# Dividing the attention output by its denominators: from transposed tiles to compacted ones with spread reciprocals

## The chip, the core and the metric

The kernel runs on one core of a Trainium2 chip. Its engines run side by side, each in the order of its own instructions: TensorE (PE) multiplies matrices and writes PSUM; VectorE (DVE) and ScalarE (ACT) read PSUM and work elementwise; GpSimd (POOL) works on SBUF; SyncE (SP) issues the DMA transfers, in order. They meet at semaphores. The metric is the device time of one execution in microseconds (us), the median of several runs.

## What is computed

One layer for 16 batches of 256 tokens with 512 features: cross attention with 32 heads of 16 features over 256 context tokens, then a feed-forward part. Cut to what matters here:

```
q = rope(layernorm(x) @ Wq);  k = rope(ctx @ Wk);  v = ctx @ Wv
w = softmax(q k^T / 4)                        # per head, 32 heads
attn = w @ v                                  # 16 x 256 x 512
x = x + tanh(g_x) * (attn @ Wout + bout)
h = square(relu(layernorm(x) @ up))
y = h @ down + (x_n @ expert) * (sum of the two largest of x_n @ gate)
out = x + tanh(g_f) * (layernorm(y) * gamma + beta)
```

All products keep about float32 accuracy: each operand is split into a rounded part (hi) and the rest (lo), and three products hi*hi, lo*hi, hi*lo are summed (`PASSES`).

## The kernel before

There are two stages: attention, batch by batch, and the feed-forward part in blocks of 512 tokens. The attention stage is a software pipeline: iteration i (from -1 to 15) has 16 steps, and in each step TensorE computes logits twice for a pair of heads: `logits_a` for batch i+1 (into pA, for the maxima, which VectorE takes and which the next step's `logits_a` waits for) and `logits_b` for batch i (into pB, transposed and with the maxima subtracted inside the product; ScalarE's Exp follows). Every second step `times_v` multiplies the exponentials of four heads by the values and a column of ones: pO then holds, for head j of the group, 16 rows of numerators at partition 32j and the denominator in row 32j+16. ScalarE copies it to `av_s` [128, 8 groups, 256] (`take_av`).

The rest of a step's work is jobs by name, from the table `SCHEDULE`; `LAG` says which batch a job works on (i+2, i+1, i or i-1) and `BANK` which of three PSUM banks (P, M, T) it uses. A bank is used by its jobs in turn: a job waits until the last one there was taken. X0 and X1 turn normalised x on TensorE, K, Q, V are projections, kT and qT turn the rotated keys and queries, m0 and m1 the maxima; O0 and O1 are the output products of the two halves of the tokens. A name with "<" is the first half of a product that is cut in two. VectorE and ScalarE empty a job's bank one step after it was computed. After K and Q, VectorE does two products with the rope tables and GpSimd adds them (`rope_sum`), before kT or qT can turn the sum. In the opening batches 0 and 1 are prepared (`OPENING`); iterations 14 and 15 have no jobs for batch i+2 left, and in iteration 15 the first tiles of the feed-forward stage are normalised and turned.

Around the change: per batch, four jobs a00, a10, a01, a11 turn `av_s` (four transposes of 128x128 each) so that tokens lie on partitions; VectorE takes the reciprocals of 16 denominators per token and multiplies them in, giving `attn`. Jobs aT0 and aT1 turn `attn` back (four transposes each), ScalarE rounds and VectorE subtracts, giving `aT` for O0 and O1. a00 stands in step 15 of its own iteration, the others in the next one.

SyncE issues per iteration: the stacks `stk` and `stq` (keys and queries laid out for the logits, four groups of six transfers), the maxima (two groups of four), x, context, the residual `xres`, and the store of x1, in the order written in `iteration` of the SyncE part. `first_loads` brings the first tiles and weights of the feed-forward stage in iteration 15.

## Time and profile before

| | |
|---|---|
| median of 3 runs | 1601.75 us (1600.06 to 1601.91) |
| the profiled execution | 1600.03 us, span 1598.2 us |
| TensorE busy | 1542.5 us (97%) |
| VectorE, ScalarE, GpSimd busy | 976.6 (61%), 638.5 (40%), 295.7 us (19%) |
| opening and iteration 0 | to 105 us |
| iterations 1 to 13 | 105 to 688 us, 44.88 us each |
| iterations 14 and 15 | 36.9 and 35.9 us |
| feed-forward stage | from 761 us |

Shares are averages over stages with different limits; a change in the attention stage is read from that stage's own rows. A timeline row has its start, its length, the instruction with what it writes and reads, the number of merged instructions, and in brackets the idle time before it with what ended it. Lengths of neighbouring TensorE rows overlap, since products are pipelined; what a job displaces is the distance between starts.

### The profile page before, as it was taken

To read this page: it belongs to the slowest core of one execution; us is meant where nothing else is said; L and a number is where in the kernel's file an instruction comes from. 1 tells how busy PE (TensorE), PEld (TensorE's weight loads), DVE (VectorE), ACT (ScalarE), POOL (GpSimd) and SP (SyncE) were. 2 spreads that over 40 slices of the span, in tenths; PEclk is the share of its full clock that TensorE was granted. 3 is DMA by queue.
4 is the path that set the end of the run, shared out by engine and by line. 5 is a ranking of instruction groups with operands and counts; after the bars stand their busy time and mean duration, and the time that the engine had idled before them with its cause. 6 is when DMAs were issued, how large, how long until landed. Compare 5 with 4: busy or idle time off the path is not lost.

```text
span 1598.2 us, 26049 instructions
## 1 busy us (share of the span) xinstructions
PE 1542.5 (97%) x9818; PEld 1157.1 (72%) x9818; DVE 976.6 (61%) x1448; ACT 638.5 (40%) x962; POOL 295.7 (19%) x370
## 2 busy tenths in 40 slices
PE   8799999999999999988999999999999999999997
PEld 6466666666666666655787887888878878788886
DVE  7887777878877777865662535436444354353524
ACT  3365555555655555566442222222222222222221
POOL 5212222222221222201010201002011020010202
PEclk9799999999999999999999999999999999999999
DMA  6644444445544334433530101101001011010101
GB/s 173 142 114 103 106 102 114 116 113 128 128 114 109 103 100 112 99 97 98 166 114 1 54 27 33 38 11 53 27 27 33 21 48 33 12 48 21 50 4 40
DMA packets 67192, 121.24 MB, mean 76 GB/s; under 512 B 12280, under 2 KB 25720, under 8 KB 67064
## 3 DMA queue, kind: packets, MB, share of 16 engines
q1 hardware_dynamic: 67064, 119.50, 27.9%
q8 instruction: 84, 1.38, 0.4%
q14 instruction: 44, 0.36, 0.1%
HBM read 51.17 MB, written 16.78 MB: 43 GB/s over the span
## 4 chain that ended last, share of the span: by engine, by line
PE 84%; DVE 11%; issue 2%; ACT 1%; POOL 1%; DMA 0%; POOLq 0%; DVEq 0%; ACTq 0%; SPq 0%
PE pP L986 16%; PE pA L1183 11%; PE pO L986 11%; PE pB L1183 11%; PE pT L986 9%; PE pO L1108 6%; PE pA L1080 6%; DVE mneg L1402 5%; PE pM L986 4%; PE pB L1096 2%; PE pT L993 2%; PE pP L993 2%; PE pM L993 2%; PE pM L1150 1%; DVE xn L1291 1%
## 5 line engine op out<-in xcount | busy, mean ns | idle before, releaser
L1402 DVE TENSOR_REDUCE mneg<-pA 128x4 f32<-128x1024 f32 x250 | 305.6, 1222 | 136.4 <-PE pA L1080 134.6
L887 ACT ACTIVATE probs<-pB 128x1024 f32<-128x1024 f32 x249 | 255.2, 1025 | 257.8 <-PE pB L1096 247.6
L1505 DVE TENSOR_TENSOR relu<-relu 128x512 f32<-128x512 f32 x128 | 88.4, 691 | 250.2 <-ACT hid L939 250.1
L704 POOL TENSOR_SCALAR var_eps<-meanvar 128x1 f32<-128x1 f32 x96 | 34.5, 360 | 1039.3 <-DVE meanvar L1287 1039.1
L1183 PE MATMUL pA<-dn,hid 128*128 128x512 f32 x768 | 196.9, 392 | 1.2 <-DVE hid L1507 1.0
L1183 PE MATMUL pB<-dn,hid 128*128 128x512 f32 x768 | 195.0, 389 | 0.0
L986 PE MATMUL pP<-fT,up 128*128 128x512 f32 x768 | 188.5, 394 | 0.0
L986 PE MATMUL pO<-fT,up 128*128 128x512 f32 x768 | 185.0, 390 | 0.0
L1183 PEld LDWEIGHTS pA<-dn,hid 128*128 128x128 f32 x768 | 143.0, 188 | 33.8 <-DVE hid L1507 4.5
L986 PEld LDWEIGHTS pO<-fT,up 128*128 128x128 f32 x768 | 143.9, 188 | 30.5 <-issue 0.5
L1183 PEld LDWEIGHTS pB<-dn,hid 128*128 128x128 f32 x768 | 144.2, 188 | 30.0
L986 PEld LDWEIGHTS pP<-fT,up 128*128 128x128 f32 x768 | 142.0, 188 | 29.8
L1080 PE MATMUL pA<-stk,stq 48*128 48x256 f32 x1000 | 127.9, 334 | 22.3 <-DVE mneg L1402 19.8
L1080 PEld LDWEIGHTS pA<-stk,stq 48*128 48x128 f32 x1000 | 76.0, 188 | 90.8 <-issue 57.8
L1108 PE MATMUL pO<-probs,v 128*17 128x256 f32 x2048 | 135.4, 382 | 2.1 <-ACT probs L887 2.1
L932 ACT ACTIVATE relu<-pO 128x512 f32<-128x512 f32 x64 | 38.3, 598 | 239.7 <-PE pO L986 239.7
L932 ACT ACTIVATE relu<-pP 128x512 f32<-128x512 f32 x64 | 38.3, 598 | 192.1 <-PE pP L986 192.1
L1096 PE MATMUL pB<-stq,stk 50*128 50x256 f32 x996 | 100.7, 280 | 0.0
L986 PE MATMUL pT<-wo,aT 128*128 128x512 f32 x384 | 99.1, 400 | 0.1
L986 PE MATMUL pT<-ex,fT 128*128 128x512 f32 x384 | 92.3, 389 | 0.0
L1507 DVE TENSOR_TENSOR hid<-relu,hid 128x512 fp32r<-128x512 f32 x128 | 88.6, 692 | 4.4
L986 PE MATMUL pP<-wq,xnT 128*128 128x512 f32 x336 | 90.6, 405 | 0.0
(199 smaller groups left out, 1972.8 us busy)
## 6 DMA issues: line engine op xcount, KB each, us to landing
stk<-kT SPq DMA_DIRECT2D x180, 128.0 KB, 2.9
stq<-qT SPq DMA_DIRECT2D x180, 128.0 KB, 3.0
fres<-x_scratch SPq DMA_DIRECT2D x34, 256.0 KB, 2.8
xin<-x SPq DMA_DIRECT2D x32, 256.0 KB, 3.0
xres<-x SPq DMA_DIRECT2D x32, 256.0 KB, 3.2
x_scratch<-xres SPq DMA_DIRECT2D x32, 256.0 KB, 2.3
out<-y_s SPq DMA_DIRECT2D x32, 256.0 KB, 2.0
fx<-x_scratch SPq DMA_DIRECT2D x29, 256.0 KB, 2.7
```

The source lines that it names most:

```text
L704: nc.gpsimd.tensor_scalar_add(var_eps[:], meanvar[:, 1:2], EPS).then_inc(ve_made, 1)
L887: nc.scalar.activation(probs[:, s % 4, :, :, :].rearrange("p a b s -> p a (b s)"), psum[:, :, :], ACT.Exp).then_inc(exp_done, 1)
L932: nc.scalar.activation(relu[m % 2][:], pU[m % 2], ACT.Relu).then_inc(relu_made, 1)
L986: last = nc.tensor.matmul(dst, lhs(a, c), rhs(w, c), start=(c == 0 and (a, w) == PASSES[0]), stop=(c == chunks_ - 1 and (a, w) == PASSES[-1]))
L993: last = nc.tensor.transpose(dst[:, c * P:(c + 1) * P], src(c), ident[:])
L1080: last = nc.tensor.matmul(psum[:, q, t * S:(t + 1) * S], st_q[par][rows, s, t * P:(t + 1) * P], st_k[par][rows, s, :], start=True, stop=True)
L1096: last = nc.tensor.matmul(psum[:, q, t * S:(t + 1) * S], st_k[par][rows, s, t * P:(t + 1) * P], st_q[par][rows, s, :], start=True, stop=True)
L1108: last = nc.tensor.matmul(pO[32 * j:32 * j + HD + 1, 0:S], v_s[par][:, t, 4 * g + j, :], probs[:, (2 * g + j // 2) % 4, j % 2, t, :], star ...
L1183: last = nc.tensor.matmul(acc[u], hid[m % 2][x_][:, u * P:(u + 1) * P], dn_s[w][:, m, :], start=(m == 0 and k == 0), stop=(m == MC - 1 and ...
L1402: nc.vector.tensor_reduce(mneg[par][:, :, 2 * u:2 * u + 2].rearrange("p t q -> p q t"), psum[:, :, :].rearrange("p q (t k) -> p q t k", t= ...
L1505: nc.vector.tensor_tensor(r[:], r[:], r[:], ALU.mult).then_inc(sq_made, 1)
L1507: nc.vector.tensor_tensor(hid[m % 2][1][:], r[:], hid[m % 2][0][:].bitcast(F32), ALU.subtract).then_inc(hid_lo, 1)
```

## The change

The division no longer goes through transposed tiles. For each batch and each half h of its groups (four groups, 16 heads):

- `gather_den`: one transfer collects the 16 heads' denominators from four partitions of `av_s` into `den` [64, 64].
- `reciprocals`: VectorE takes the reciprocal, rounds it and subtracts (den_hi, den_lo), at step 14 for the first half and step 3 of the next iteration for the second.
- `scatter_recips`: two transfers lay both parts out as 32 rows of 256 (`recips`).
- Job b0 or b1: two TensorE products of `spread`, a 0/1 tile made once on GpSimd in the opening (`make_spread`), with `recips`, which puts each head's reciprocal on the 16 partitions of its features.
- `move_av`: four transfers compact the numerators of `av_s` into `numer` (128 partitions, no gaps).
- VectorE multiplies b's bank into `numer`, ScalarE rounds (`round_av`, steps 4 and 8) and GpSimd subtracts (`rest_av`), giving `aT_hi` and `aT_lo`, which O0 and O1 use. The rows of Wout are permuted on the host to match.

The jobs a00, a10, a01, a11, aT0 and aT1 are gone. V1 moves from step 11 to step 4 and to bank T; O0 from steps 8 and 9 to 9 and 11, O1 from 13 to 13 and 15. GpSimd's order gets `rest_av` ahead of Q0's and of Q1's sum, the residual between. SyncE's order changes: `first_loads` stands before the second half's gather, the second part of stq after the residual, the store of the second x1 tile in the next iteration. In the first feed-forward block b0 stands at m = 0, b1 at m = 2, O0 and O1 at m = 3 and 4.

```diff
 SCHEDULE = {
-    0: ("X0", "a10"),
+    0: ("X0",),
-    2: ("Q0<", "a01"),
+    2: ("Q0<", "b0"),
...
+RECIPROCALS = {14: 0, 3: 1}
+ROUNDED = {4: 0, 8: 1}
...
+R_AT = HALF_ROWS
+R_ROWS = 2 * NH // 2
+MOVES = 4
...
-        attn = [sb1(f"attn{t}", [P, D]) for t in range(TT)]
-        aT = [sb1(f"aT{i}", [P, KC, P], F32R) for i in range(2)]
+        numer = under("numer", [P, KC, S])
+        aT_lo = sb1("aT_lo", [P, KC, S], F32R)
+        aT_hi = sb1("aT_hi", [P, KC, S], F32R)
...
-        rden = [sb1(f"rden{i}", [P, NH // 2]) for i in range(2)]
+        den = under("den", [HALF_ROWS, S // 4])
+        den_lo = sb1("den_lo", [HALF_ROWS, S // 4], F32R)
+        den_hi = sb1("den_hi", [HALF_ROWS, S // 4], F32R)
...
+        recips = low[0][R_AT:R_AT + R_ROWS, :]
+        spread = low[1][R_AT:R_AT + R_ROWS, :].rearrange("r (c p) -> r c p", c=2)
...
+            def gather_den(b, h):
+                sp.wait_ge(av_taken, GROUPS * b + GROUPS // 2 * (h + 1))
+                if some(2 * b + h):
+                    sp.wait_ge(rc_in, 2 * INC * (2 * b + h))
+                sp.dma_start(den[:, :], av_s[HD:P:32, GROUPS // 2 * h:GROUPS // 2 * (h + 1), :]
+                             .rearrange("j g (r s) -> j (g r) s", r=4)).then_inc(den_in, INC)
+            def scatter_recips(b, h):
+                sp.wait_ge(rc_made, 3 * (n + 1))
+                if some(n):
+                    freed, of = ("b0", b) if h else ("b1", b - 1)
+                    sp.wait_ge(done[BANK[freed]], number(freed, of))
+                for k, part in enumerate((den_hi, den_lo)):
+                    sp.dma_start(recips[NH // 2 * k:NH // 2 * (k + 1), :].bitcast(F32), part[:, :].bitcast(F32)).then_inc(rc_in, INC)
+            def move_av(b, h):
+                sp.wait_ge(av_taken, GROUPS * b + GROUPS // 2 * (h + 1))
+                if some(b):
+                    sp.wait_ge(done[BANK["O1"]], number("O1", b - 1))
+                for j in range(MOVES):
+                    sp.dma_start(numer[j:P:4, 2 * h:2 * h + 2, :].rearrange("p c s -> p (c s)"),
+                                 av_s[32 * j:32 * j + HD, GROUPS // 2 * h:GROUPS // 2 * (h + 1), :]
+                                 .rearrange("d g s -> d (g s)")).then_inc(moved[h], INC)
...
+                if within(bt):
+                    move_av(bt, 0)
+                if ending:
+                    first_loads()
                 if within(b1) and not opened("kT1", b1):
                     load_stack(b1, (par + 1) % 2, 1, "k")
+                if within(bt):
+                    gather_den(bt, 1)
+                if within(bt - 1):
+                    store_x1(bt - 1, 1)
+                if within(bt):
+                    move_av(bt, 1)
+                    scatter_recips(bt, 1)
+                if within(i):
+                    load_max(i, par % 2, 1)
+                if within(bt):
+                    load_residual(bt)
...
+                gather_den(i, 0)
...
+                scatter_recips(i, 0)
...
+            def rest_av(b, h):
+                pool.wait_ge(at_hi, 2 * b + h + 1)
+                nc.gpsimd.tensor_tensor(aT_lo[:, cut, :], numer[:, cut, :], aT_hi[:, cut, :].bitcast(F32),
+                                        ALU.subtract).then_inc(at_lo, 1)
...
+            def round_av(b, h):
+                act.wait_ge(taken[BANK[f"b{h}"]], number(f"b{h}", b))
+                nc.scalar.copy(aT_hi[:, cut, :], numer[:, cut, :]).then_inc(at_hi, 1)
...
-                    u = int(name[1])
-                    pe.wait_ge(av_taken, GROUPS * b + GROUPS // 2 * (t + 1))
-                    last = turn(psum, lambda c: av_s[:, GROUPS // 2 * t + c, u * P:(u + 1) * P])
+                    pe.wait_ge(rc_in, 2 * INC * (2 * b + t + 1))
+                    for c in range(2):
+                        last = nc.tensor.matmul(psum[:, c * S:(c + 1) * S], spread[:, c, :], recips,
+                                                start=True, stop=True)
...
-                    nc.vector.reciprocal(r[:], heads[:, :, HD]).then_inc(rd_made, 1)
...
+                    dve.wait_ge(moved[t], MOVES * INC * (b + 1))
+                    nc.vector.tensor_tensor(numer[:, cut, :], psum.rearrange("p (c s) -> p c s", c=2), numer[:, cut, :],
+                                            ALU.mult).then_inc(freed, 1)
+            def reciprocals(b, h):
+                n = 2 * b + h
+                dve.wait_ge(den_in, INC * (n + 1))
+                nc.vector.reciprocal(d, d).then_inc(rc_made, 1)
+                nc.vector.tensor_copy(den_hi[:, :], d).then_inc(rc_made, 1)
+                nc.vector.tensor_tensor(den_lo[:, :], d, den_hi[:, :].bitcast(F32), ALU.subtract).then_inc(rc_made, 1)
...
+                    if s in RECIPROCALS and within(i - RECIPROCALS[s]):
+                        reciprocals(i - RECIPROCALS[s], RECIPROCALS[s])
```

Three places in the new order. SyncE at the boundary between two full iterations (stk, stq: stacks; mT, low: maxima; xres: residual; x_scratch: stored x1). Before, from the maxima of m0 on, over the boundary:

```order
L526 DMA stq<-mT 1x8x256 x4
L517 DMA stq<-qT 16x2x1024 x6
L542 DMA x_scratch<-xres 128x512
L517 DMA stk<-kT 16x2x1024 x6
L517 DMA stq<-qT 16x2x1024 x6
L498 DMA xin<-x 128x512
L537 DMA xres<-x 128x512 x2
L526 DMA stq<-mT 1x8x256 x4
L498 DMA xin<-x 128x512
```

And after, from the same place:

```order
L577 DMA stq<-low 1x8x256 x4
L540 DMA stq<-qT 16x2x1024 x6
L560 DMA low<-den_hi 16x4x64
L560 DMA low<-den_lo 16x4x64
L568 DMA numer<-av_s 32x1x512 x4
L540 DMA stk<-kT 16x2x1024 x6
L549 DMA den<-av_s 64x1x64
L593 DMA x_scratch<-xres 128x512
L568 DMA numer<-av_s 32x1x512 x4
L560 DMA low<-den_hi 16x4x64
L560 DMA low<-den_lo 16x4x64
L577 DMA stq<-low 1x8x256 x4
```

Two scatters and four moves now stand ahead of the next iteration's stk, and the gather of the second half's denominators behind it.

VectorE from the statistics in step 2 to Q0's rotation in step 4 (mneg: maxima, L1402 before and L1516 after). Before:

```order
L1282 BN_STATS stats<-xin 128x6
L1287 BN_AGGR meanvar<-stats 128x2
L1402 TENSOR_REDUCE mneg<-pA 128x2x2
L1347 RECIPROCAL rden<-pT 128x16
L1349 TENSOR_TENSOR attn<-pT,rden 128x256
L1291 TENSOR_SCALAR xn<-xin,meanvar,rstd 128x512
L1402 TENSOR_REDUCE mneg<-pA 128x2x2
L1333 TENSOR_TENSOR mT<-pM,mT 16x256
L1327 TENSOR_TENSOR rot_q<-pP,cos_t 128x512
L1330 TENSOR_TENSOR rot<-pP,sin_t 128x512
```

After:

```order
L1393 BN_STATS stats<-xin 128x6
L1398 BN_AGGR meanvar<-stats 128x2
L1516 TENSOR_REDUCE mneg<-pA 128x2x2
L1454 TENSOR_TENSOR numer<-pT,numer 128x512
L1402 TENSOR_SCALAR xn<-xin,meanvar,rstd 128x512
L1462 RECIPROCAL den<-den 64x64
L1464 CAST den_hi<-den 64x64
L1466 TENSOR_TENSOR den_lo<-den,den_hi 64x64
L1516 TENSOR_REDUCE mneg<-pA 128x2x2
L1444 TENSOR_TENSOR low<-pM,low 16x256
L1438 TENSOR_TENSOR rot_q<-pP,cos_t 128x512
L1441 TENSOR_TENSOR rot<-pP,sin_t 128x512
```

The product into numer takes the place of a reciprocal and a product; the three denominator operations stand between the normalisation and the maxima of step 4.

SyncE in iteration 15, around the first loads of the feed-forward stage. Before:

```order
L542 DMA x_scratch<-xres 128x512
L537 DMA xres<-x 128x512 x2
L595 DMA g_gamma<-gamma 128x512
L596 DMA g_beta<-beta 128x512
L597 DMA gt_raw<-gate 128x4x8
L599 DMA fx<-x_scratch 128x512
L599 DMA fres<-x_scratch 128x512 x2
L599 DMA relu<-x_scratch 128x512
L582 DMA y_s<-up 128x4x128 x4
```

After:

```order
L560 DMA low<-den_lo 16x4x64
L568 DMA numer<-av_s 32x1x512 x4
L661 DMA g_gamma<-gamma 128x512
L662 DMA g_beta<-beta 128x512
L663 DMA gt_raw<-gate 128x4x8
L665 DMA fx<-x_scratch 128x512
L665 DMA fres<-x_scratch 128x512 x2
L665 DMA relu<-x_scratch 128x512
L648 DMA y_s<-up 128x4x128 x4
L549 DMA den<-av_s 64x1x64
L593 DMA x_scratch<-xres 128x512
L568 DMA numer<-av_s 32x1x512 x4
```

The residual has gone behind, four moves stand ahead, and the gather, the scatter and the maxima of m1 follow the loads.

## Rows read from the trace of the kernel before

**Rows 1.** Windows; columns as named: stretch, engines' busy us, granted clock, DMA share.

```profile
core 0: us, PE busy (x) PEld busy (x) DVE busy (x) ACT busy (x) POOL busy (x), PEclk, DMA share, GB/s
40.00:80.00 40.00, 28.73 (x185) 19.13 (x183) 32.31 (x37) 12.55 (x20) 12.05 (x13) 0.74 0.68 142
...
419.12:464.00 44.88, 43.88 (x382) 29.69 (x382) 35.63 (x51) 25.36 (x36) 11.20 (x12) 1.00 0.45 114
688.41:725.32 36.91, 32.27 (x320) 20.56 (x321) 24.98 (x30) 22.04 (x30) 2.52 (x2) 1.00 0.35 95
725.32:761.26 35.94, 29.64 (x291) 17.71 (x291) 20.24 (x38) 24.37 (x37) 5.70 (x10) 1.00 0.36 106
```

**Rows 2.** Timeline of TensorE in iteration 7 and 8: start, length in us, instructions.

```profile
405.99 0.66 PE L993 MATMUL pT<-ident,attn 128*128 128x128 f32 x4
406.40 1.64 PE L986 MATMUL pM<-wv,ctx 128*128 128x512 f32 x6
407.97 0.50 PE L1080 MATMUL pA<-stk,stq 48*128 48x256 f32 x4
...
409.63 0.39 PE L1058 MATMUL pM<-ident,mneg 128*16 128x128 f32 x2
409.85 0.60 PE L993 MATMUL pP<-ident,rot_q 128*128 128x128 f32 x4
...
417.96 0.66 PE L993 MATMUL pM<-ident,av_s 128*128 128x128 f32 x4
419.12 0.50 PE L1080 MATMUL pA<-stk,stq 48*128 48x256 f32 x4 [0.50 <-DVE mneg L1402]
...
427.20 0.60 PE L993 MATMUL pT<-ident,av_s 128*128 128x128 f32 x4
427.73 0.50 PE L1080 MATMUL pA<-stk,stq 48*128 48x256 f32 x4
...
431.76 0.66 PE L993 MATMUL pT<-ident,av_s 128*128 128x128 f32 x4
432.35 0.50 PE L1080 MATMUL pA<-stk,stq 48*128 48x256 f32 x4
...
433.43 0.66 PE L993 MATMUL pP<-ident,xn 128*128 128x128 f32 x4 [0.35 <-DVE rot L1330]
```

**Rows 3.** Timeline of TensorE in iteration 0: kT1.

```profile
90.44 0.63 PE L993 MATMUL pM<-ident,rot_k 128*128 128x128 f32 x4 [0.47 <-POOL rot_k L711]
```

**Rows 4.** Timeline of VectorE, iteration 8, steps 0 and 3 to 5.

```profile
420.80 0.25 DVE L1347 RECIPROCAL rden<-pM 128x16 f32<-128x16 f32 x1
...
430.04 0.67 DVE L1291 TENSOR_SCALAR xn<-xin,meanvar,rstd 128x512 f32<-128x512 f32 x1
430.64 1.23 DVE L1402 TENSOR_REDUCE mneg<-pA 128x4 f32<-128x1024 f32 x1
...
433.31 1.20 DVE L1402 TENSOR_REDUCE mneg<-pA 128x4 f32<-128x1024 f32 x1
```

**Rows 5.** Timeline of SyncE's issues, end of iteration 7: start, issue time, transfers.

```profile
412.50 2.72 SPq L526 DMA_DIRECT2D stq<-mT  x4
415.41 3.79 SPq L517 DMA_DIRECT2D stq<-qT  x6
```

**Rows 6.** Landing times in us of the stk transfers issued from 400 to 470 us.

```profile
DMA to landing us min/median/max: 2.5/2.9/3.9
```

**Rows 7.** Transfers issued from 720 to 745 us: count, size, median us to landing.

```profile
gt_raw<-gate SPq DMA_DIRECT2D x1, 16.0 KB, 6.3
```

**Rows 8.** Timeline of TensorE in iteration 15: the first feed-forward tile's turn.

```profile
736.58 0.66 PE L993 MATMUL pP<-ident,fx 128*128 128x128 f32 x4 [1.25 <-DVE fx L1291]
```

**Rows 9.** Timeline of VectorE in iteration 15: the statistics of that tile.

```profile
733.81 0.67 DVE L1282 BATCH_NORM_STATS2 stats<-fx 128x6 f32<-128x512 f32 x1
```

**Rows 10.** Timeline of SyncE's issues in iteration 15: the first loads.

```profile
725.58 0.33 SPq L595 DMA_DIRECT2D g_gamma<-gamma  x1
...
729.52 3.52 SPq L582 DMA_DIRECT2D y_s<-up  x4
```

More of the change, by code:

```diff
@@ L67 @@
 SCHEDULE = {
-    0: ("X0", "a10"),
+    0: ("X0",),
     1: ("K0",),
-    2: ("Q0<", "a01"),
+    2: ("Q0<", "b0"),
     3: ("m1", "Q0"),
-    4: ("a11",),
+    4: ("V1",),
     5: ("X1", "kT0"),
-    6: ("aT0",),
+    6: ("b1",),
     7: ("K1", "Q1<"),
-    8: ("Q1", "O0<"),
-    9: ("kT1", "O0"),
+    8: ("Q1",),
+    9: ("kT1", "O0<"),
     10: ("qT0",),
-    11: ("aT1", "V1"),
+    11: ("O0",),
     12: ("m0", "qT1"),
-    13: ("O1",),
+    13: ("O1<",),
     14: ("V0",),
-    15: ("a00",),
+    15: ("O1",),
 }
@@ L109 @@
 CUT = [x[:-1] for names in SCHEDULE.values() for x in names if x[-1] == "<"]
-TWO_STEP = ("X0", "X1", "qT0", "qT1", "kT0", "kT1", "aT0", "aT1", "m0", "m1")
+TWO_STEP = ("X0", "X1", "qT0", "qT1", "kT0", "kT1", "m0", "m1")
 ROPES = ("K0", "Q0", "K1", "Q1")
-A_JOBS = ("a00", "a10", "a01", "a11")
+R_AT = HALF_ROWS
+R_ROWS = 2 * NH // 2
+MOVES = 4
 X_AT = (6, 8, 10, 12)
@@ L219, in sb1, with under @@
             return first.enter_context(nc.sbuf_tensor(name, shape, dt))
+        def under(name, shape):
+            with nc.sbuf_tensor(name, shape, F32) as tile:
+                return tile
         wq_s = [sb1(f"wq{i}", [P, KC, D], F32R) for i in range(2)]
@@ L570, in iteration, with load_raw @@
                     load_stack(b2, par % 2, 0, "q")
[L571 to L575 removed]
+                scatter_recips(i, 0)
+                if ending:
+                    load_w(ffn_chunks[6])
+            def load_raw(start, end):
+                for k in range(start, end):
                     sp.dma_start(raw1[k], chunks[k][0]).then_inc(w_raw[k], INC)
@@ L736, in iteration @@
                 if prepares:
-                    for name in ROPES[1:]:
-                        rope_sum(b2, name)
+                    rope_sum(b2, "K1")
+                ending = isinstance(i, int) and i == B - 1
+                if ending:
+                    for u in range(2):
+                        inv_std(NT + u + 1)
+                if within(bt):
+                    rest_av(bt, 1)
+                if prepares:
+                    rope_sum(b2, "Q1")
                 if within(i + 3):
@@ L741, in iteration @@
                     split_ctx(i + 3, (par + 1) % 2)
-                if isinstance(i, int) and i == B - 1:
-                    for u in range(UT):
+                if ending:
+                    for u in range(2, UT):
                         inv_std(NT + u + 1)
@@ L1206, in fblock @@
                     if first_block and m == 0:
-                        job("a01", B, B)
                         pe.wait_ge(gt_lo, 1)
@@ L1464, in _ @@
             phase1(dve, iteration, ahead=1)
-            job("a00", B - 1)
+            job("O1", B - 1)
             split_gate()
-            job("a10", B)
             dve.wait_ge(av_done, GROUPS * B)
```

137 lines of the change are left out of this document (83 added, 54 removed), and 8 rows, old and new, of tables (BANK, LAG).

## Prediction

> **What bounds the kernel now.** I read the windows view first, one stretch per kind of iteration [rows 1]. An iteration with all its work (there are 13, numbers 1 to 13) takes 44.88 us; TensorE is busy for 43.88 of them at a granted clock of 1.00, VectorE for 35.63, GpSimd for 11.20. So TensorE bounds these 13, and what it no longer does there is gained, unless a wait takes its place. Iteration 14 (36.91 us) and 15 (35.94 us) have no projections to do; TensorE is busy for 32.27 and 29.64 us in them and waits for VectorE's chain. The TensorE timeline then gives what each removed job displaces and where TensorE waits today [rows 2, 3]; the VectorE and SyncE timelines give the pace of the two engines that the new path runs through [rows 4, 5]; the last views give transfer times and the end of the attention stage [rows 6 to 10].
>
> **TensorE: removed.** Per batch six jobs of four transposes go. What a job costs is the distance from its start to the next start. It is 0.53 for a01 (427.20 to 427.73) and likewise for a10, 0.41 for aT1 (405.99 to 406.40), 0.66 for a00 (417.96 to 419.12 less the 0.50 wait), 0.59 for a11 (431.76 to 432.35) and likewise for aT0. Sum 3.3 us. Two waits of TensorE beside these jobs go with them: 0.50 after a00 and 0.35 before X1, 0.85 together [rows 2].
>
> **TensorE: added.** Two jobs of two products with a 32-row stationary tile and 256 columns. Nothing like it is in the trace. Below it lies the pair of m transposes (409.63 to 409.85, 0.22), above it a job of four transposes with 0.53 [rows 2]; I take 0.35, between them, so 0.7 per iteration. Cut products and V1 only change place. TensorE's work would then need 44.88 - 3.3 - 0.85 + 0.7 = 41.4 us.
>
> **New wait 1: kT1.** The first half of O0 leaves step 8, where it stood between K1's rope and kT1. Iteration 0, which has no O0 yet, shows what is then late: kT1 waited 0.47 us for GpSimd's rope sum [rows 3]. I add 0.47.
>
> **New wait 2: the denominators.** VectorE now takes the second half's denominators at step 3, and it works strictly in its order: behind that wait stand the maxima of step 4, the split of m1 and both rotations of Q0, for which TensorE's X1 waits. When is VectorE there? Step 3 began 8.61 us after the iteration (419.12 to 427.73); without a10 and a01 and with one new job that is 7.9. The normalisation xn started 2.3 us into the step (430.04) behind a reciprocal and a product that one product replaces, and takes 0.6 [rows 2, 4]: VectorE is ready at 10.85.
>
> When is the transfer there? SyncE issues in order. The write of m0's maxima started 6.62 us before the iteration's end (412.50 to 419.12) [rows 2, 5]; the halves of O1 trade places at no cost, but a00 and its wait (1.16) no longer stand in between, so 5.5. From there SyncE issues the four maxima in 2.9 (412.50 to 415.41), six pieces of stq in 3.9 (3.79 and a gap), then what is new ahead of the gather: two scatters of reciprocals and four moves at 0.63 each, the issue time of such a transfer between SBUF tiles (3.79/6), with gaps 4.0; then six pieces of stk, 3.9 like those of stq [rows 5]. That is 14.7: the gather is issued 9.2 us into the iteration. Its landing is unknown. Pieces of stk land 2.5 to 3.9 us after issue, median 2.9 [rows 6]; the gather is 16 KB against 128 KB but in 64 pieces, so I take 2.7: it lands at 11.9, and VectorE waits 1.05 us.
>
> From there: three small VectorE operations at 0.27 (0.25 and a gap, the reciprocal of rows 4), 0.8; maximum, m1 split and Q0's rotations 2.67 (430.64 to 433.31) [rows 4]; so X1 is released at 15.4. TensorE would reach it at 14.2: today at 13.96 (433.43 less 0.35, less 419.12), less a10, a01 and a11 (1.65), plus the new job (0.35) and V1 (as V1 today from 406.40 to 407.97, 1.57) [rows 2]. The wait is 1.2 us.
>
> An iteration then takes 41.4 + 0.47 + 1.2 = 43.1 us, 1.8 less than now; 13 of them give **-23 us**.
>
> **The Trainium skill on this gather.** The Trainium skill, "DMA: Bandwidth & Descriptors", section "Anatomy of one DMA — SWDGE (gpsimd) path", gives a fixed cost of about 2.0 us plus bytes over 436 GB/s, on another engine's path; an estimate by it is 2.04 us, a wait of 0.5 and some 1576 us in all, but no piece of stk landed in under 2.5 [rows 6]. The same page, section "Why a DMA increments its semaphore by 16 and not by 1", says that a transfer uses the largest number of engines up to 16 that divides the slowest dimension of both sides. That speaks against this gather (64 rows from 4: four engines with 16 pieces each); no row shows such a transfer, and it stands behind the third rival.
>
> **Other parts at nothing.** VectorE loses four reciprocals, four half products and two splits and gains two full products and six small operations; with 35.63 of 44.88 it has room except at step 3. ScalarE's two copies become two others of the same shape. GpSimd's two subtractions stand ahead of Q0's and Q1's rope sums; it is busy for 11.20 of 44.88 us, and each sum is wanted several steps later. If that cover goes, kT1's wait grows one for one. The moves land by about 7.5 and 15.5 us into the iteration, against uses at 9.6 and 20. SyncE issues 14 more transfers, about 9 us, in time when it waited. b1 at step 6 needs the scatter, issued when the reciprocals end (12.7) and landed near 16, against 17. The spread tile is built on GpSimd in the opening, where that engine is busy for 12.05 of 40 us [rows 1].
>
> **The end of the attention stage.** In iteration 14 the six jobs less the two new ones are worth at most 2.6, but steps without projections come sooner while the gather doesn't, and VectorE waits at step 3 for about 3 us: +0.5. In iteration 15 the gather stands behind the first loads of the feed-forward stage: 11 transfers issued over 7.5 us (725.58 to 733.04), now behind four moves too, so it is issued about 10.3 us into the iteration. In that queue even a 16 KB transfer took 6.3 us to land [rows 7, 10]; I take 4.8, so 15.1. Behind the wait stand the statistics of the first feed-forward tile, and TensorE's turn of it, which waits for them today (736.58, 11.3 us in, after 1.25 idle) [rows 8]. From denominators to that turn: 0.8 for the reciprocals, 0.3 for the split of m1 and 2.8 from the start of the statistics to the turn as today (733.81 to 736.58) [rows 8, 9]; it moves to 19.0, **+7.7**. VectorE's evacuation of O0 leaves the chain of tiles and the late O1 and b0 lengthen its end; I set the two against each other. TensorE idles for some 7 us here. In the stretch from 40 to 80 us, where it waited most, the granted clock was 0.74 against 1.00 [rows 1], a mix of 1.2 and 2.4 GHz; for this I add 0.8.
>
> The first feed-forward block is all TensorE and loses four jobs, each a little cheaper than aT1's 0.41 [rows 2], and gains one: -1.1.
>
> **Sum,** against the profiled execution's 1600.03 us: -23 + 0.5 + 8.5 - 1.1 = -15, **1585**. The median of the runs is 1.7 above the profiled execution, so I predict **1586**.
>
> **Rivals.**
> 1. *The gather is early.* If the small transfers are issued faster than 0.63 (loads from memory take less) or land in 2 us, X1's wait falls to 0.1: 42.0 us per iteration, 13 x 2.9 = 37 saved: 1571. For it: 16 KB is little. Against it: every SBUF transfer in the trace cost the same 0.63.
> 2. *The end stays hidden.* The gather in iteration 15 passes the loads on other engines and lands 3 us after issue: 2 to 3 us better, 1582. It lies in the forecast's range.
> 3. *Slower: the gather is late in every iteration.* The gain of 13 iterations just pays for the 8 us at the end when an iteration takes 44.3, that is when the gather lands 3.9 us after issue. At 5 us an iteration takes 45.3: 1600 + 13 x 0.4 + 8 + 2 = 1615. For it: 64 pieces of 256 B behind six of 128 KB. Against it: 3.9 is the longest landing that [rows 6] shows for a larger transfer.
> 4. *It does not free TensorE.* If the new jobs cost as much as transposes (0.53) and K1's wait doubles, the iteration takes 44.0: 1597, no change that can be seen.
>
> **How the numbers follow.** Forecast with rival 2: 0.55, landing between 2.2 and 3.4, 1577 to 1594. Rival 1: 0.18. Rival 3: 0.17, rival 4: 0.10. About 0.2% (3 us) is what a measurement of this kernel can tell from none. Faster collects the forecast, rival 1 and a little of rival 4: 0.76; same 0.09; slower 0.15. Leaving out half of rival 3's tail and the far end of rival 1, the range is 1568 to 1605.
>
> **What would show it.** In the trace after: iterations 1 to 13 near 43.1 us; TensorE waiting at X1 for VectorE about 1.2 us and at kT1 for GpSimd about 0.5; VectorE's reciprocal at step 3 waiting for the gather about 1 us; iteration 15 near 44 us with one wait of VectorE of some 7 us. I am wrong if SyncE is held at a wait I take as long met, since all that is queued behind it would then shift, or if VectorE does not wait for the gather at all.

## The result and the profile after

The changed kernel took 1632.2 us (median of four runs, 1626.67 to 1638.34) against 1601.2 for the kernel before: ratio 1.0195, 95% interval 1.0158 to 1.0232. It is slower by 31 us where 15 us less was forecast. The profiled execution took 1626.67 us with a span of 1624.9, 26.7 more than before. Where these lie, counted from V0 to V0 (the start of V0's product, step 14) and then to the first product of the feed-forward stage:

| stretch | before | after | forecast | measured |
|---|---|---|---|---|
| opening and iteration 0 | 101.53 | 100.51 | 0 | -1.0 |
| the 13 full iterations | 583.45 | 582.46 | -23 | -1.0 |
| iteration 14 | 36.93 | 43.70 | +0.5 | +6.8 |
| iteration 15, to the first product | 39.35 | 58.97 | +8.5 | +19.6 |
| feed-forward stage, to the end | 837.0 | 839.2 | -1.1 | +2.3 |

(In the forecast's column the 8.5 are 7.7 and 0.8 for the clock.)

The windows of after, one stretch per kind of iteration (columns as in [rows 1]): two of the slow full iterations, an ordinary one, iteration 14, and iteration 15 to the first product.

```profile
100.51:147.07 46.56, 42.05 (x358) 27.14 (x355) 36.44 (x48) 25.51 (x37) 13.54 (x14) 0.96 0.50 117
236.72:283.63 46.91, 43.57 (x364) 28.21 (x361) 36.94 (x49) 25.54 (x37) 13.54 (x14) 0.96 0.51 122
460.00:504.07 44.07, 42.15 (x364) 27.52 (x360) 35.86 (x49) 25.53 (x37) 13.59 (x14) 1.00 0.54 130
682.97:726.67 43.70, 36.95 (x305) 22.05 (x301) 25.54 (x29) 21.98 (x31) 5.06 (x4) 0.80 0.41 95
726.67:785.64 58.97, 35.83 (x293) 20.85 (x289) 22.26 (x41) 27.33 (x42) 8.13 (x12) 0.77 0.32 89
```

Before, every full iteration took 44.9 us at a clock of 1.00. After, they take from 43.5 to 47.1, and three of the 13 show a clock of 0.96. TensorE is busy for less than in [rows 1] (42.15 against 43.88), so it was freed; it now waits.

**An ordinary iteration.** TensorE in the iteration from 460.00 on: b0, then the three waits.

```profile
471.62 0.50 PE L1177 MATMUL pT<-low 32*128 32x256 f32 x2
472.05 0.51 PE L1193 MATMUL pA<-stk,stq 48*128 48x256 f32 x4
...
478.18 0.50 PE L1193 MATMUL pA<-stk,stq 48*128 48x256 f32 x4 [0.43 <-DVE mneg L1516]
...
479.69 0.66 PE L1102 MATMUL pP<-ident,xn 128*128 128x128 f32 x4 [0.78 <-DVE rot L1441]
...
491.29 0.63 PE L1102 MATMUL pM<-ident,rot_k 128*128 128x128 f32 x4 [0.47 <-POOL rot_k L801]
```

VectorE at step 3 of it, and SyncE's issues (start, issue time, transfers):

```profile
474.33 0.61 DVE L1402 TENSOR_SCALAR xn<-xin,meanvar,rstd 128x512 f32<-128x512 f32 x1
475.97 0.55 DVE L1462 RECIPROCAL den<-den 64x64 f32<-64x64 f32 x1 [1.02 <-DMA den<-av_s]
...
476.77 0.22 DVE L1466 TENSOR_TENSOR den_lo<-den,den_hi 64x64 fp32r<-64x64 f32 x1
476.91 1.21 DVE L1516 TENSOR_REDUCE mneg<-pA 128x4 f32<-128x1024 f32 x1
```

```profile
469.59 3.78 SPq L540 DMA_DIRECT2D stk<-kT  x6
473.49 0.61 SPq L549 DMA_DIRECT2D den<-av_s  x1
```

The chain is the predicted one, and its sizes are right: the step 0 logits start 3.84 us behind V0 here, so VectorE is ready at 11.1 us into the iteration (predicted 10.85), the gather is issued at 9.65 (9.2), the reciprocal starts at 12.1 (11.9), VectorE waits 1.02 us (1.05). TensorE pays 0.43 at the maxima and 0.78 at X1, 1.21 in all (1.2). kT1 waits 0.47, as in [rows 3].

**A slow one.** The same place in the iteration from 236.72 on: VectorE, GpSimd, TensorE.

```profile
253.37 0.55 DVE L1462 RECIPROCAL den<-den 64x64 f32<-64x64 f32 x1 [1.70 <-DMA den<-av_s]
...
254.17 1.20 DVE L1466 TENSOR_TENSOR den_lo<-den,den_hi 64x64 fp32r<-64x64 f32 x1
255.30 1.21 DVE L1516 TENSOR_REDUCE mneg<-pA 128x4 f32<-128x1024 f32 x1
```

```profile
254.02 1.27 POOL L786 TENSOR_TENSOR aT_lo<-numer,aT_hi 128x512 fp32r<-128x512 f32 x1 [2.63 <-ACT aT_hi L965]
```

```profile
256.56 0.50 PE L1193 MATMUL pA<-stk,stq 48*128 48x256 f32 x4 [2.08 <-DVE mneg L1516]
```

TensorE in the windows behind that wait (stretch, busy us, granted clock, DMA share, GB/s):

```profile
256.72:259.22 2.50, 1.72 (x16) 0.89 0.09 20
259.22:261.72 2.50, 2.50 (x22) 0.50 0.26 80
261.72:264.22 2.50, 2.50 (x22) 0.92 0.95 284
```

The gather is issued 0.6 us later here (14.1 us behind V0 against 13.5); SyncE took 4.63 us for stk's six pieces instead of 3.78. That alone would be a wait of 1.1 us for TensorE, as e5 below shows. But den_lo, 0.22 us elsewhere, takes 1.20: it ends as GpSimd's subtraction for the first half (254.02 + 1.27) ends. TensorE idles 2.08 us, and behind that its clock is at half, 1.2 instead of 2.4 GHz, for about 3.5 us.

**The end.** SyncE in iteration 15, then VectorE, GpSimd and TensorE at the first feed-forward tile:

```profile
736.90 3.30 SPq L648 DMA_DIRECT2D y_s<-up  x4
740.34 1.82 SPq L549 DMA_DIRECT2D den<-av_s  x1
...
747.13 0.60 SPq L560 DMA_DIRECT2D low<-den_hi  x1
...
748.41 2.81 SPq L577 DMA_DIRECT2D stq<-low  x4
751.35 0.83 SPq L588 DMA_DIRECT2D xres<-x  x2
```

```profile
746.01 0.54 DVE L1462 RECIPROCAL den<-den 64x64 f32<-64x64 f32 x1 [8.81 <-DMA den<-av_s]
...
747.28 0.67 DVE L1393 BATCH_NORM_STATS2 stats<-fx 128x6 f32<-128x512 f32 x1
748.49 0.18 DVE L1398 BATCH_NORM_AGGREGATE meanvar<-stats 128x2 f32<-128x6 f32 x1 [0.53 <-DVE stats L1393]
757.49 0.55 DVE L1402 TENSOR_SCALAR fx<-fx,meanvar,rstd 128x512 f32<-128x512 f32 x1 [8.82 <-POOL rstd L796]
```

```profile
754.14 2.48 POOL L829 TENSOR_TENSOR xres<-xres,gbout 128x512 f32<-128x512 f32 x2 [12.80 <-DMA xres<-x]
...
756.89 0.57 POOL L796 TENSOR_TENSOR rstd<-var_eps,neg_half 128x1 f32<-128x1 f32 x1
```

```profile
758.09 1.11 PE L1102 MATMUL pP<-ident,fx 128*128 128x128 f32 x4 [18.72 <-DVE fx L1402]
```

VectorE waits twice, 8.8 us each time. The first wait is for the gather behind the first loads, as predicted. The second was not seen: the statistics are there at 748.67, but rstd of that tile (the reciprocal of its standard deviation, which the normalisation needs) stands on GpSimd behind the two residual adds of batch 14. Their load stands last on SyncE, behind the first loads, the moves, the scatter and the maxima; before, it stood ahead of the first loads, 1.3 us behind V0 instead of 24.7:

```profile
723.24 1.98 SPq L537 DMA_DIRECT2D xres<-x  x2
```

Against [rows 8], where TensorE waited 1.25 us for this tile, it waits 18.72, and from 758 to 771 us its granted clock is 0.51.

### The profile page after: what moved, and what is told of

Same layout as the page of the kernel before. It is cut to its first block, busy times and chain, and to the rows that moved or that the text cites. A ratio compares the mean times of both kernels' runs of the same rounds, so it can differ in the third digit from the quotient of the medians.

```text
span 1624.9 us, 25920 instructions
## 1 busy us (share of the span) xinstructions
PE 1530.4 (94%) x9498; PEld 1132.6 (70%) x9498; DVE 985.7 (61%) x1416; ACT 640.3 (39%) x962; POOL 338.1 (21%) x406
## 4 chain that ended last, share of the span: by engine, by line
PE 65%; SPq 13%; DVE 12%; DMA 3%; issue 3%; POOL 2%; ACT 1%; DVEq 0%; POOLq 0%; ACTq 0%
PE pP L1095 12%; PE pA L1296 11%; PE pB L1296 11%; PE pO L1095 10%; PE pT L1095 8%; SPq L540 7%; DVE mneg L1516 5%; PE pA L1193 3%; PE pO L1221 3%; SPq L577 2%; DMA den<-av_s 2%; SPq L568 2%; PE pM L1102 2%; PE pP L1102 2%; PE pM L1095 2%
## 5 line engine op out<-in xcount | busy, mean ns | idle before, releaser
L1516 DVE TENSOR_REDUCE mneg<-pA 128x4 f32<-128x1024 f32 x250 | 305.8, 1223 | 114.0 <-PE pA L1193 111.5
L1221 PE MATMUL pO<-probs,v 128*17 128x256 f32 x2048 | 141.2, 395 | 1.1 <-ACT probs L994 1.1
L1095 PE MATMUL pT<-wo,aT_hi 128*128 128x512 f32 x256 | 97.5, 423 | 0.2 <-DVE xres L1448 0.2
```

The costliest lines, as they stand in the source:

```text
L1095: last = nc.tensor.matmul(dst, lhs(a, c), rhs(w, c), start=(c == 0 and (a, w) == PASSES[0]), stop=(c == chunks_ - 1 and (a, w) == PASSES[-1]))
L1221: last = nc.tensor.matmul(pO[32 * j:32 * j + HD + 1, 0:S], v_s[par][:, t, 4 * g + j, :], probs[:, (2 * g + j // 2) % 4, j % 2, t, :], star ...
L1516: nc.vector.tensor_reduce(mneg[par][:, :, 2 * u:2 * u + 2].rearrange("p t q -> p q t"), psum[:, :, :].rearrange("p q (t k) -> p q t k", t= ...
```

## The experiments

Each is the changed kernel with the edit shown, from e7 on one upon the other; ratios are to the kernel before, run on the same chip (1600.1 to 1601.6 us).

| kernel | median us (range) | ratio (95% interval) |
|---|---|---|
| e1_gather_early | 1600.1 (1597.9 to 1602.1) | 0.9997 (0.9987 to 1.0006) |
| e2_rstd_first | 1629.9 (1625.7 to 1633.4) | 1.0192 (1.0167 to 1.0217) |
| e3_gather_before_loads | 1639.5 (1632.7 to 1646.4) | 1.0231 (1.0204 to 1.0257) |
| e4_all_three | 1591.0 (1590.6 to 1593.9) | 0.9948 (0.9931 to 0.9964) |
| e5_round_later | 1622.8 (1620.0 to 1625.3) | 1.0145 (1.0126 to 1.0165) |
| e6_gather_later | 1712.1 (1709.8 to 1714.6) | 1.0701 (1.0682 to 1.0720) |
| e7_end | 1588.8 (1587.4 to 1592.8) | 0.9927 (0.9909 to 0.9944) |
| e8_end_swap | 1580.7 (1579.8 to 1583.3) | 0.9877 (0.9859 to 0.9894) |
| e8_again | 1582.6 (1581.9 to 1584.9) | 0.9880 (0.9863 to 0.9896) |
| e9_whole | 1604.7 (1603.1 to 1607.0) | 1.0021 (1.0011 to 1.0030) |

**The gather's place in full iterations.**

```
                 if ending:
                     first_loads()
-                if within(b1) and not opened("kT1", b1):
-                    load_stack(b1, (par + 1) % 2, 1, "k")
                 if within(bt):
                     gather_den(bt, 1)
+                if within(b1) and not opened("kT1", b1):
+                    load_stack(b1, (par + 1) % 2, 1, "k")
```

> Edit: in full iterations the gather of the second half's denominators is issued ahead of the six pieces of stk, 3.9 us sooner; in the last iteration it still stands behind the first loads. Theory A (the gather's place costs it): in the changed kernel VectorE waits 0.45 to 1.85 us for the gather in each of iterations 1 to 13 and 4.02 us in iteration 14; TensorE's wait for the maxima follows (0.3 to 2.3 us), and behind waits of 2 us or more its granted clock reads 0.50 for about 4 us (iterations 1, 4, 11). With the gather 3.9 us sooner all three go: full iterations of 43.2 to 43.5 us without exception instead of 43.5 to 47.1, iteration 14 some 5 us shorter, together 1632 - 15 - 5 = 1610 to 1614 us. Theory B (the SBUF transfers themselves crowd the queues, DMA share 0.54 against 0.45): stk and the moves then come later by what the gather gains, waits only change their names and the time stays within 5 us of 1632.

Measured: 32 us less than the changed kernel, more than theory A had (the two traces differ by 24.6: 22.5 in the full iterations, 4.5 in iteration 14, less 1.2 each in iteration 15 and the feed-forward stage). Nine of the 13 full iterations take 42.95 to 43.0 us, the others 42.7 to 44.1 (together 559.98); TensorE waits 0.84 us in most of them: kT1 0.47, K1 0.19, X1 0.17. VectorE no longer waits at step 3, and no iteration but the last shows it waiting for a gather:

```profile
459.71 0.61 DVE L1402 TENSOR_SCALAR xn<-xin,meanvar,rstd 128x512 f32<-128x512 f32 x1
460.25 0.53 DVE L1462 RECIPROCAL den<-den 64x64 f32<-64x64 f32 x1
```

Iteration 14 takes 39.2 us instead of 43.7. Theory B falls: the transfers still hold a DMA share of 0.55 in these iterations, and the waits did not just change their names. Some small new ones are left: b1 waits up to 0.45 us in iterations 11 to 13, and in iteration 4 kT1 waits 1.58 us for GpSimd's sum, which stands behind residual adds that waited 6.94 us for their load. The one edit brings the kernel level with the kernel before; the end still costs the whole gain (iteration 15: 60.2 us).

**GpSimd's order at the end.**

```
+                    ending = isinstance(i, int) and i == B - 1
+                    if ending:
+                        inv_std(NT + 1)
                     for t in range(TT):
                         pool.wait_ge(res_in[t], INC * (bt + 1))
                         nc.gpsimd.tensor_tensor(xres[t][:], xres[t][:], gbout[:], ALU.add).then_inc(res_made, 1)
...
                 if ending:
-                    for u in range(2):
-                        inv_std(NT + u + 1)
+                    inv_std(NT + 2)
```

> Edit: in the last iteration GpSimd takes the reciprocal deviation of the first feed-forward tile ahead of the two residual adds of batch 14; nothing else. Theory A (GpSimd's order is what holds the end): in the changed kernel the statistics of that tile end at 748.67, and its rstd only at 757.46, since GpSimd stands at the residual adds, whose loads SyncE issues last (751.35) and which end at 756.6. With the edit rstd follows the statistics at about 749.5, the tile's turn on TensorE comes at 750.5 instead of 758.1: 7 to 8 us less, 1624 to 1625. Theory B (the prediction's: VectorE's wait of 8.8 us for the gather is the whole price of the end): the adds are off the path and the time stays at 1632 within 2 us.

Measured: the stretch of iteration 15 is 52.0 us instead of 58.97, 7.0 less, as theory A has it. GpSimd, then TensorE:

```profile
755.75 0.57 POOL L796 TENSOR_TENSOR rstd<-var_eps,neg_half 128x1 f32<-128x1 f32 x1
760.56 2.98 POOL L832 TENSOR_TENSOR xres<-xres,gbout 128x512 f32<-128x512 f32 x2 [4.24 <-DMA xres<-x]
```

```profile
756.95 1.12 PE L1104 MATMUL pP<-ident,fx 128*128 128x128 f32 x4 [11.01 <-DVE fx L1404]
```

The whole kernel is only 2.3 us faster than the changed one, and the expected 1624 was missed: two of its full iterations took 49.5 and 50.8 us, by the late gather, den_lo and the clock. Which of the full iterations are slow differs from trace to trace of the same order, so the verdict rests on the stretch and not on the total.

**The gather ahead of the first loads, in the last iteration alone.**

```
                 if ending:
+                    gather_den(bt, 1)
                     first_loads()
...
-                if within(bt):
+                if within(bt) and not ending:
                     gather_den(bt, 1)
```

> Edit: in the last iteration alone the gather is issued ahead of the first loads of the feed-forward stage, about 6.5 us sooner; GpSimd's order stays. Theory A (the end hangs on GpSimd's residual adds, whose load stands on SyncE behind first loads, moves, scatter and maxima): VectorE's wait for the gather falls from 8.8 to 2 us or less, but the load of the residual is issued only as much sooner as SyncE no longer waits at the scatter for the reciprocals (751.35 to about 748), so the tile's turn comes some 3 us sooner: 1628 to 1630. Theory B (VectorE's wait is the price): 6 to 8 us less, 1624 to 1626.

Measured: VectorE waits for no gather any more in iteration 15, and the stretch is 58.0 us instead of 58.97; theory A had 3 us. Its total is the slowest of the three for the same reason as above (five full iterations of 49 to 51 us). SyncE's load of the residual, then VectorE at the tile, waiting for GpSimd:

```profile
770.87 0.83 SPq L588 DMA_DIRECT2D xres<-x  x2
```

```profile
776.76 0.55 DVE L1403 TENSOR_SCALAR fx<-fx,meanvar,rstd 128x512 f32<-128x512 f32 x1 [13.37 <-POOL rstd L797]
```

The wait that the prediction put at the centre of the end is worth 1 us by itself. Without it the load is issued 23.3 us behind V0 instead of 24.7, so it isn't the gather's wait that makes this load late, but the issues that stand ahead of it; the adds start 1.7 us sooner, and rstd and the turn with them.

**The three together.** The diffs of the three, one upon the other.

> Edit: the gather ahead of stk in every iteration and ahead of the first loads in the last one, and GpSimd's rstd of the first tile ahead of the residual adds. Theory A: the gains of the two places add up: 15 to 20 us from iterations 1 to 14 and 15 to 18 from the end (the last iteration's tile is turned at about 13 us into the iteration instead of 27.6), so 1632 - 35 = 1594 to 1602, level with the kernel before or a little under it. Theory B (crowded queues): no more than 8 us less, 1624 or above.

Measured 1591.0, 41 us less than the changed kernel and 9 less than the kernel before. The first tile is turned 13.8 us into iteration 15 (the iteration starts at 703.26), the stretch is 49.65 us:

```profile
717.04 1.12 PE L1105 MATMUL pP<-ident,fx 128*128 128x128 f32 x4 [4.92 <-DVE fx L1405]
```

The two edits of the end are worth 1 and 7 us alone, 9.3 together, and 10.6 against e1's 60.2. Two paths lead to the turn, side by side: gather, reciprocals, statistics; and load, residual adds, rstd. The later one counts. The turn comes 27.6 us into the iteration as changed, 26 with the first path mended alone (e3), 19.9 with the second alone (e2). No run put the residual's load itself back ahead of the first loads.

**GpSimd's subtraction away from den_lo.**

```
-ROUNDED = {4: 0, 8: 1}
+ROUNDED = {5: 0, 8: 1}
```

> Edit: the changed kernel with one number other: ScalarE's rounding of the first half, and with it GpSimd's subtraction behind it, stand at step 5 instead of step 4. Seen in the traces so far: VectorE's den_lo takes 0.22 us, but 1.20 to 1.28 where it starts while GpSimd's subtraction (17.3 to 18.6 us after V0's start) runs, which is when VectorE waited 1.35 us or more for the gather; TensorE then waits 2.08 us or more for the maxima, and its granted clock reads 0.50 for 4 to 13 us. Theory A (the two engines' operations on SBUF shut each other out, and the long waits are a late gather plus that): without the neighbour den_lo stays at 0.22, no wait for the maxima in iterations 2 to 13 is above 1.5 us, the clock stays at 1.00 there, iterations take 43.5 to 45 us: 1632 - 9 = 1618 to 1625. Theory B (the late gather alone makes the long waits): den_lo or the operation in its place is as long, iterations of 46 to 51 us stay, 1626 to 1638.

Measured 1622.8, as theory A has it. In the iteration that begins at 236.2 VectorE waited 1.70 us, as in the slow one above, and TensorE behind it 1.10 instead of 2.08:

```profile
252.84 0.55 DVE L1462 RECIPROCAL den<-den 64x64 f32<-64x64 f32 x1 [1.70 <-DMA den<-av_s]
...
253.64 0.22 DVE L1466 TENSOR_TENSOR den_lo<-den,den_hi 64x64 fp32r<-64x64 f32 x1
```

```profile
255.05 0.51 PE L1193 MATMUL pA<-stk,stq 48*128 48x256 f32 x4 [1.10 <-DVE mneg L1516]
```

No den_lo or den_hi is above 0.3 us in the 14 iterations; in the changed kernel five of these 56 operations took 1.20 to 1.28. Eleven of the 13 full iterations lie between 43.5 and 44.7 us. One point of theory A fell: iteration 11 (45.7) still lost clock, behind a wait of only 0.93 us, and so did iteration 1 (47.1), behind 0.98.

**The gather 3.2 us later.**

```
-                if within(bt):
-                    gather_den(bt, 1)
                 if within(bt - 1):
                     store_x1(bt - 1, 1)
                 if within(bt):
                     move_av(bt, 1)
+                    gather_den(bt, 1)
                     scatter_recips(bt, 1)
```

> Edit: the changed kernel with the gather of the second half issued 3.2 us later, behind the store and the four moves. Theory A (lost clock is part of the price of a late gather): VectorE's wait becomes 3.6 to 5 us, TensorE's wait for the maxima 3 to 4.5 us in every iteration, and behind each the granted clock reads 0.50 for 4 us or more, which costs 2 us or more of work at half speed: iterations of 48 to 52 us, 13 x 5 = 65 us and more: 1690 to 1730. Theory B (the price is linear, as the prediction's chain has it): 3.2 us later makes 3.2 us more, no clock is lost: iterations of 47 us, 1632 + 13 x 2.8 = 1665 to 1675.

Measured 1712.1, 80 us more than the changed kernel. Full iterations take 48.0 to 52.8 us (mean 50.9 against 44.8): waits of TensorE are 5.0 us per iteration against 2.4, and its work between waits 45.95 us against 42.38, the same instructions. So of the 6.1 us that are added per iteration 2.5 are waits and 3.6 are lost clock: theory A. No den_lo is held up here (0.22 us in every iteration): a late gather alone costs clock when it is late enough. TensorE behind a wait of 3.92 us, and the window behind it (columns as in [rows 1]):

```profile
173.89 0.50 PE L1192 MATMUL pA<-stk,stq 48*128 48x256 f32 x4 [3.92 <-DVE mneg L1515]
```

```profile
177.00:182.00 5.00, 5.00 (x36) 2.84 (x34) 2.56 (x4) 2.14 (x4) 1.79 (x2) 0.50 0.65 170
```

**The rest of the end.** On top of e4: the four tiles first among the first loads, and the second tile's rstd ahead of the residual adds too.

```
+                for u in range(UT):
+                    sp.dma_start(first_fx[u][:], x1_d[u]).then_inc(first_in[u], INC)
                 sp.dma_start(g_gamma[:], gamma.partition_broadcast(P)).then_inc(f_small, INC)
...
-                        inv_std(NT + 1)
+                        for u in range(2):
+                            inv_std(NT + u + 1)
...
```

> Edit: the kernel with all three edits (gather ahead of stk and of the first loads, rstd of the first tile ahead of the residual adds), and beside that the four tiles ahead of gamma, beta and gate in the first loads, and the second tile's rstd ahead of the residual adds too. In that kernel TensorE still waited 4.92 us for the first tile (its load landed 5.5 us after issue) and 3.97 for the second (its rstd stood 3.9 us at GpSimd behind the residual adds). Theory A (GpSimd's order and the queue ahead of the tiles): the second wait goes but for 0.5, the first falls by 1 to 1.5 us, the clock lost in this stretch a little less: 1591 - 6 = 1583 to 1587. Theory B (TensorE has too little to do there, whatever waits last): under 2 us, 1589 to 1591.

Measured 1588.8, between the two theories, and its gain over e4 isn't sure: the ranges overlap. The waits went as theory A says (3.45 and 0.53 us for the two tiles), but a third took their place: b1 waited 3.77 us for the scatter (its second part was issued at 722.55 and landed 2.5 us later), which stands behind the weights, and those took 5.55 us to issue instead of 3.50.

```profile
712.38 5.55 SPq L649 DMA_DIRECT2D y_s<-up  x4
...
721.90 0.60 SPq L560 DMA_DIRECT2D low<-den_hi  x1
```

```profile
725.12 0.76 PE L1179 MATMUL pT<-low 32*128 32x256 f32 x2 [3.77 <-issue]
```

**Cover for kT1.** On top of e7:

```
-    9: ("kT1", "O0<"),
+    9: ("O0<", "kT1"),
```

> Edit: the kernel before in this list, and at step 9 the first half of O0 ahead of kT1 instead of behind it. Theory A (kT1 waits 0.47 us for GpSimd's rope sum in each iteration because nothing stands ahead of it): the first half of O0 (1.3 us) covers that, iterations of 42.95 become 42.5, 13 x 0.47 = 6 us less than the kernel before in this list: 1577 to 1581. Theory B (the wait only moves on, to the maxima or kT1's evacuation): within 2 us of it.

Measured 1580.7, as theory A has it, and 1582.6 beside the last kernel: some 19 us below the kernel before. Full iterations take 42.5 us, 6.1 less for the 13 than in e7's trace, and kT1 waits no more; in most of them 42.1 us of work and 0.36 of waits are left.

> The kernel with the swap at step 9 once more, unchanged, beside the one with whole pieces on the same chip: 1580 to 1582 us, iterations of 42.5 us. Theory A puts the other kernel 4 us below it, theory B level with it.

**Fewer pieces.** On top of e8:

```
-    8: ("Q1",),
-    9: ("O0<", "kT1"),
+    8: ("Q1", "O0<"),
+    9: ("kT1",),
...
-    13: ("O1<",),
+    13: (),
...
-                        job("O1<", B, B)
                         job("O1", B, B)
```

> Edit: the kernel with the swap at step 9, with fewer pieces between jobs of other shapes: the first half of O0 directly behind Q1 (step 8), and O1 whole at step 15 instead of two halves. In the traces so far a half product of 128 rows takes 1.57 to 1.60 us to the next start where logits or b0 follow, and 1.46 to 1.49 where another product does; O1 whole took 2.96, its halves 1.57 each. Theory A (each change to a smaller stationary tile costs TensorE 0.1 us, so that cutting a job is not free): 0.1 for Q1 and 0.2 for O1, iterations of 42.5 become 42.2, 13 x 0.3 = 4 us less than that kernel. Theory B (TensorE's count is the same and only the steps' lengths differ; VectorE then waits in the long step and TensorE behind it): no change within 2 us, or longer.

Measured 1604.7: 22 us more (17.8 of it in the full iterations), so longer, as theory B allows, but by another wait than it names. The pieces did get cheaper: counted by the distance to the next start, the products of O0 and O1 fall from 6.27 to 6.03 us per iteration and those of Q from 6.21 to 6.10. But the next step's `logits_a` waits for the maxima of this step, and that round takes 1.83 us, however little else the step has to do. TensorE waits 1.58 us per iteration for it: 1.09 at step 14, behind step 13, now without a job, and 0.50 at step 10, behind the short step 9. VectorE isn't behind with its work, since it waits for the logits first. TensorE at steps 13 and 14, then VectorE in between:

```profile
448.36 0.50 PE L1195 MATMUL pA<-stk,stq 48*128 48x256 f32 x4
...
450.19 0.50 PE L1195 MATMUL pA<-stk,stq 48*128 48x256 f32 x4 [1.09 <-DVE mneg L1517]
```

```profile
448.91 1.23 DVE L1517 TENSOR_REDUCE mneg<-pA 128x4 f32<-128x1024 f32 x1 [0.53 <-PE pA L1195]
```

Iterations take 44.0 us.

## Why the prediction was wrong

Between the forecast and the profiled execution lie 42 us: 22 in the full iterations, 6 in iteration 14, 11 in iteration 15, 3 in the feed-forward stage (the opening gave 1 back).

**Right:** the removed jobs (3.3 us per iteration, none left), kT1's wait (0.47), the two chains up to VectorE at step 3 and up to the gather, the wait of 1.05 and its price of 1.2 in an ordinary iteration, and in iteration 15 VectorE's wait (8.8 against "some 7": the gather was issued 9.8 us into the iteration, predicted 10.3, and landed at 15.5, predicted 15.1). GpSimd's subtractions delayed kT1 by nothing more. None of the rivals happened as told: in full iterations the gather landed 2.3 to 2.5 us after the start of its issue, which is neither rival 1's 2 nor rival 3's 5 but the forecast's own condition (2.2 to 3.4), and the time lies beyond even rival 3's 1615. So the transfer was sized rightly, and what hangs on it was not.

**The full iterations** were forecast at 43.1 us and take 44.80. That is 41.4 + 0.47 + 1.2 against 42.38 of work and 2.43 of waits. Four terms failed:

1. *"Cut products and V1 only change place."* Cutting has a price. Before, O1 stood in one piece; after, it is two of 1.58 to 1.60 each. TensorE before, then one half after:

```profile
455.92 3.04 PE L986 MATMUL pT<-wo,aT 128*128 128x512 f32 x12
458.88 0.50 PE L1080 MATMUL pA<-stk,stq 48*128 48x256 f32 x4
```

```profile
418.75 0.50 PE L1095 MATMUL pT<-wo,aT_hi 128*128 128x512 f32 x1
...
420.33 0.51 PE L1193 MATMUL pA<-stk,stq 48*128 48x256 f32 x4
```

   2.96 became 3.2. Likewise Q0's first piece and Q1's second now end ahead of b0 and of logits, 1.59 us each, where they ended ahead of another job of 128 rows with 1.49 and 1.50. All this is 0.35 for the O products (5.98 to 6.33 us) and 0.2 for the Q products (5.99 to 6.20) per iteration. e9 gave 0.35 of it back. The Trainium skill, "TensorEngine Tiling (Array Packing)", section "Key Properties", says that a change of the tiling mode drains TensorE. The rows agree, if the 48 rows of the logits and the 32 of b0 count as another mode; they show about 0.1 us for it, and no run tells a drain from another cost of the change.

2. *b0 and b1 at 0.35 each:* 0.43 (471.62 to 472.05), 0.16 per iteration.

3. *The wait taken as one number.* SyncE's issues scatter (six pieces took 3.7 to 5.2 us before as well; why, no run shows), so that "every SBUF transfer in the trace cost the same 0.63" did not hold, and the gather is the last of some 20. VectorE's wait for it ran from 0.45 to 1.85 us, and its four longest (1.61 us and more) made VectorE run into GpSimd's subtraction, which the prediction put "at nothing" because GpSimd is busy for 11.20 of 44.88 us. Busy share says nothing on this: GpSimd's subtraction held VectorE's operation up to its own end. e5 shows it. In the three kernels whose full iterations are the same (after, e2, e3) all 13 waits of TensorE of 2.08 us or more stand behind such a held operation, and no shorter wait for the maxima does. Of the 0.76 us that the waits lie above the forecast's 1.67, some 0.15 are K1's wait (0.19 us in ten of the 13 iterations), which the sum doesn't have, and 0.09 are a wait of 1.17 us at the start of iteration 1. The Trainium skill, "SBUF — State Buffer", section "SBUF: two separate sides", says that VectorE and GpSimd share a pair of ports, and that whichever of a VectorE operation in a two-port mode, or with two SBUF inputs (this only against a GpSimd operation that reads SBUF), and a GpSimd operation starts first holds it to its end. The trace agrees: den_lo, with both inputs in SBUF, goes from 0.22 to 1.20 and more, while products with an input in PSUM took 0.68 beside GpSimd and alone.

4. *The clock.* The prediction counted lost clock at the end alone. After iteration 4's wait of 2.08 us the work between waits came to 43.57 us instead of 42.1. In after, e2 and e3, 11 of the 13 waits of 2.08 us or more (2.31 the longest) were followed by a granted clock of 0.5, and 2 of 21 shorter ones; behind each of the 13 stood X1's wait, 0.30 to 0.79 us. One such fall cost from 1.4 to 5.8 us of work. That fits the spread of the runs, 12 us for the changed kernel and 3 to 4 for e1, e4 and e8, though each has only one trace.

In sum: the waits are 0.76 us per iteration above the 1.67 forecast, the clock takes 0.37 (42.38 of work against e1's 42.01), pieces and b jobs 0.61 (42.01 against 41.4): the 1.7 us that were missed. e1 takes 43.08 us, the forecast's figure, but only because it has no wait for the gather.

**Iteration 14** (+0.5 forecast): VectorE waited 4.02 us, where "about 3" was taken to be paid by shorter steps. It was not, and the clock fell to 0.80 over the iteration: TensorE's work between waits came to 37.1 us against 32.4 before, with six jobs less and two small ones more. e1 takes away 4.5 of the 6.8 us; without any wait for the gather it still shows a clock of 0.91 there, and what began that fall stays open.

**Iteration 15** (+8.5 forecast): the failed step is "2.8 from the start of the statistics to the turn as today". It took 10.8 us (747.28 to 758.09), and 3.1 in e2. The way runs through GpSimd, whose queue was looked at in full iterations only. Its residual adds wait for a load that SyncE now issues last, and that path ends later than the one through the gather, whether the gather is late or not (e3). With GpSimd's order mended and nothing else (e2) the tile is turned 19.9 us into the iteration; the prediction had 19.0. The clock's price was put at 0.8; from 758 to 771 us half of it was missing, some 6 us by an estimate from that window (11.6 us of TensorE's work at 0.51).

**The feed-forward stage** (-1.1 forecast): its first block waits 1.8 us for ScalarE and VectorE that it did not wait for before, and its first 25 us have a granted clock of 0.93, where it was 1.00. No run took this apart; e8 is as long (840.3 us from its first product against 837.0), with 2.8 us of such waits and no lost clock. What is left of the end in e8 (iteration 15 47.1 us against 39.35) was not settled either.

## What to carry to other kernels

When a step is moved into an in-order queue, walk down every queue that its consumers share, not only the engine that waits: here the new order put the residual's load last on SyncE, the load held GpSimd's adds, and these held the statistics' next step and with it the next stage. Where two paths meet, mending one gives only what the other leaves. A transfer that an in-order engine waits for goes ahead of the bulk transfers in its queue; one swap was worth 32 us here. A step can't be made shorter than its round of logits and maxima (e9), so cutting a product also fills a step. And a wait near the edge is to be costed with its scatter: what it meets when it is longer (another engine's hold on SBUF, the clock) makes the price rise by steps.

## What the runs showed of the hardware

- VectorE's den_lo (64x64, both inputs in SBUF): 0.22 us alone, 1.20 to 1.28 where it started during GpSimd's subtraction; den_hi, a cast, 0.2 and 1.23.
- TensorE's clock fell to 1.2 GHz behind waits of 2.08 to 2.31 us, with a second one of 0.30 to 0.79 soon after, in 11 of 13 cases, and four times behind waits of 0.75 to 0.98 (e2, e3, e5); with waits of 3.2 to 4.1 us in every iteration (e6) 3.6 us of each iteration were lost to it.
- Six matmuls of 128x512 took TensorE 1.58 to 1.60 us to the next start where they stood alone between jobs of other shapes, and 1.45 to 1.51 with a product of their shape ahead or another job of 128 rows and columns behind.
- A gather of 16 KB in 64 pieces between SBUF tiles was there 2.3 to 2.5 us after the start of its issue, beside 128 KB transfers with a median of 2.9; behind the moves (e6) 2.0 to 2.2, behind the first loads 5.7.
